# Local attention's projections as three bfloat16 products, with the lookback scores before the phrase keys

## The reference, cut to what matters

```
h = layernorm(x)
q = h @ q_w.T + q_b;  k = h @ k_w.T + k_b;  v = h @ v_w.T + v_b
ph = running mean of h within chunks of 32 tokens      # the phrase state
pk = ph @ pk_w.T + pk_b;  pv = ph @ pv_w.T + pv_b
scores of q against the tokens before it; top 16 of them, with the token just before once more,
    and one phrase score, of q against pk of the token before
w = softmax over these 18;  out = weighted sum of v and pv
x = x + out
```

## Time and profile before

| | |
|---|---|
| median of three runs | 2538.76 us |
| the profiled execution's own time | 2541.76 us |
| its span, first to last instruction | 2539.8 us |
| mean granted TensorE clock over the span | 0.955 of full |
| PE busy | 2312.9 us (91%) |
| DVE, ACT, POOL busy | 1826.2, 1557.3, 1123.5 us |
| first instruction of `local1` | 2375.35 us |
| end of its last instruction (line 2739) | 2474.85 us |

### The profile page before, as it was taken

One profiled execution on the slowest core, in us unless ns is written; L12 is line 12 of the kernel. 1 busy time (PEld: TensorE's weight loads), 2 busy tenths in 40 slices (PEclk: granted clock), 3 DMA queues, 4 the chain that ended last, 5 costly groups with the idle time before them and its releaser, 6 DMA issues. The chain is left out here.

```text
span 2539.8 us, 57508 instructions
## 1 busy us (share of the span) xinstructions
PE 2312.9 (91%) x21955; PEld 1499.9 (59%) x21955; DVE 1826.2 (72%) x3370; ACT 1557.3 (61%) x2912; POOL 1123.5 (44%) x895
## 2 busy tenths in 40 slices
PE   5799999999999999998888699995799899998795
PEld 3346656666566655666445577772567676776442
DVE  7478877888788867776363699995777777766236
ACT  4347666666666666665234499883377676887313
POOL 4437666666666665554100000004367676656100
PEclk8899999999999999998899799997999999999897
DMA  6223233224222321124321699984533434224002
GB/s 212 52 71 93 84 106 83 75 75 125 82 70 79 107 72 42 42 60 152 113 104 39 219 368 364 365 301 165 163 110 118 127 121 127 88 89 161 30 1 85
DMA packets 256273, 313.56 MB, mean 123 GB/s; under 512 B 71792, under 2 KB 183024, under 8 KB 255104
## 3 DMA queue, kind: packets, MB, share of 16 engines
q1 hardware_dynamic: 252048, 301.76, 37.1%
q10 hardware_dynamic: 3312, 6.03, 0.6%
q0 software_dynamic: 640, 2.10, 0.3%
HBM read 226.23 MB, written 47.91 MB: 108 GB/s over the span
## 5 line engine op out<-in xcount | busy, mean ns | idle before, releaser
L816 POOL TENSOR_TENSOR a_plo<-a_p,a_phi 128x512 bf16<-128x512 f32 x272 | 316.0, 1162 | 358.9 <-ACT a_phi L870 358.1
L1074 PE MATMUL ps<-w,a_xhi 128*128 128x512 bf16 x1088 | 413.9, 380 | 6.0 <-PEq L3010 6.0
L1075 PE MATMUL ps<-w,a_xhi 128*128 128x512 bf16 x1088 | 413.8, 380 | 0.0
L1076 PE MATMUL ps<-w,a_xlo 128*128 128x512 bf16 x1088 | 413.8, 380 | 0.0
L2234 POOL TENSOR_TENSOR a_plo<-a_p,a_phi 128x512 bf16<-128x512 f32 x256 | 306.6, 1198 | 178.8 <-ACT a_phi L2271 169.7
L838 ACT ACTIVATE a_kraw<-ps 128x256 f32<-128x256 f32 x272 | 104.2, 383 | 373.5 <-PE ps L1076 371.8
L2366 DVE CUSTOM_DVE_ANT_0 a_junk<-ps,a_biasrow 128x512 bf16<-128x512 f32 x256 | 176.2, 688 | 117.6 <-PE ps L2506 114.6
L893 DVE TENSOR_TENSOR a_v<-ps,a_v 128x256 bf16<-128x256 f32 x272 | 114.3, 420 | 164.3 <-ACT a_v L840 162.8
L2266 ACT ACTIVATE a_p<-ps,a_mcol 128x512 f32<-128x512 f32 x256 | 174.8, 683 | 87.6 <-PE ps L2524 79.9
L907 DVE SCALAR_TENSOR_TENSOR a_kraw<-a_kraw,a_rn 128x1024 f32<-128x1024 f32 (+1 forms) x80 | 154.2, 1928 | 78.3 <-POOL a_rn L781 78.3
L781 POOL TENSOR_TENSOR a_rn<-a_rn,a_power 128x16 f32<-128x16 f32 (+1 forms) x80 | 204.0, 2550 | 6.6
(11 more groups left out here) (461 smaller groups left out, 6890.6 us busy)
## 6 DMA issues: line engine op xcount, KB each, us to landing
e_wst<-in_L_ffn_W SPq DMA_DIRECT2D x46, 2048.0 KB, 10.3
a_ks<-a_khi SPq DMA_DIRECT2D x256, 64.0 KB, 2.0
a_ks<-a_klo SPq DMA_DIRECT2D x256, 64.0 KB, 2.1
a_ct<-in_ctxT SPq DMA_DIRECT2D x16, 1024.0 KB, 6.3
a_ks<-k1h_d SPq DMA_DIRECT2D x128, 128.0 KB, 2.5
xa<-in_ctx SPq DMA_DIRECT2D x8, 1024.0 KB, 5.6
k1h_d<-a_khi SPq DMA_DIRECT2D x64, 128.0 KB, 2.1
k1l_d<-a_klo SPq DMA_DIRECT2D x64, 128.0 KB, 1.7
```

Source lines behind the costliest of these rows:

```text
L816: pool.tensor_tensor(p_lo[:, m % 3, :], p32[:, m % 2, :], p_hi[:, m % 3, :], ALU.subtract)\
L1074: pe.matmul(out, x_hi[:, c, tile], w_hi[:, c, g, :], start=(c == 0), stop=False)
L1075: pe.matmul(out, x_hi[:, c, tile], w_lo[:, c, g, :], start=False, stop=False)
L1076: last = pe.matmul(out, x_lo[:, c, tile], w_hi[:, c, g, :], start=False, stop=(c == C - 1))
```

## The change

Only `local1` changes.

- Every float32 operand of the projections is split into a high and a low bfloat16 tile: all five weights (`w_hi`, `w_lo`), the turned `Hn` (`ht_hi`, `ht_lo`) and the phrase state (`pt_hi`, `pt_lo`). ACT makes the high tiles (five copies of 128x2048, eight of 128x512), DVE the four `ht_lo` straight from PSUM, POOL the five `w_lo` of 128x2048 and the four `pt_lo` of 128x512.
- The 12 feature groups and the 8 value groups are 12 bfloat16 matmuls of 128x512 each. Scores, turns and outputs stay float32.
- PE's order becomes: queries, keys, lookback scores, phrase keys, phrase scores, four values, the turns of the weights, the first phrase value, four outputs' first halves, and then each further phrase value followed by the second half of the output before it.
- Values use banks 2 and 3 alone. DVE's masking and top 16 follow the lookback scores directly; the phrase scores' part stands behind them. DVE's copies of values and additions into `X` are spread along.

```diff
+        @block.gpsimd
+        def _(pool):
+            def weight_low(k):
+                pool.wait_ge(whi_done, k + 1)
+                pool.tensor_tensor(w_lo[:, k], w[k], w_hi[:, k], ALU.subtract).then_inc(wlo_done, 1)
+
+            for k in range(3):
+                weight_low(k)
+            for c in range(C):
+                pool.wait_ge(pthi_done, c + 1)
+                pool.tensor_tensor(pt_lo[:, c, :], PT_[:, c, :], pt_hi[:, c, :], ALU.subtract).then_inc(ptlo_done, 1)
+            for k in range(3, 5):
+                weight_low(k)
...
         @block.scalar
-            norm.scalar(act)
-            turn.scalar(act, ps, HT)
-            act.wait_ge(c_in, 7 * 16)
-            for n in range(3 * C):
+            def weight_high(k):
+                act.wait_ge(w_in[k], 16)
+                act.activation(w_hi[:, k], w[k], ACT.Copy).then_inc(whi_done, 1)
...
+            weight_high(0)
+            norm.scalar(act)
+            weight_high(1)
+            for c in range(C):
+                act.wait_ge(h_tp, c + 1)
+                act.activation(ht_hi[:, c, :], ps[:, c, :], ACT.Copy).then_inc(hthi_done, 1)
+            weight_high(2)
+            act.wait_ge(c_in, 7 * 16)
+            for n in range(C):
+                feature(n)
+                act.wait_ge(pf_cp, n + 1)
+                act.activation(pt_hi[:, n, :], PT_[:, n, :], ACT.Copy).then_inc(pthi_done, 1)
+            for n in range(C, 2 * C):
+                feature(n)
+                if n < C + 2:
+                    weight_high(3 + n - C)
+            for n in range(2 * C, 3 * C):
+                feature(n)
...
         @block.vector
             norm.vector(dve, step, Hn, X)
+            for c in range(C):
+                dve.wait_ge(hthi_done, c + 1)
+                dve.tensor_tensor(ht_lo[:, c, :], ps[:, c, :], ht_hi[:, c, :], ALU.subtract).then_inc(htlo_done, 1)
...
-            dve.wait_ge(s_mm, 2)
+            dve.wait_ge(s_mm, 1)
             (masking, two rounds of max and match_replace, r1)
+            dve.wait_ge(s_mm, 2)
             (phrase scores, m_ready)
+            value(0)
             dve.wait_ge(e_done, 2 * B)
...
         @block.tensor
+            def features(k):
+                pe.wait_ge(wlo_done, k + 1)
+                if k == 2:
+                    pe.wait_ge(ptlo_done, C)
+                hi, lo = (ht_hi, ht_lo) if k < 2 else (pt_hi, pt_lo)
+                for o in range(C):
+                    n = C * k + o
+                    if n >= 2:
+                        pe.wait_ge(f_cp, n - 1)
+                    out, cols = ps[:, 4 + n % 2, :], slice(o * P, (o + 1) * P)
+                    for c in range(C):
+                        pe.matmul(out, w_hi[:, k, c, cols], hi[:, c, :], start=(c == 0), stop=False)
+                        pe.matmul(out, w_hi[:, k, c, cols], lo[:, c, :], start=False, stop=False)
+                        last = pe.matmul(out, w_lo[:, k, c, cols], hi[:, c, :], start=False, stop=(c == C - 1))
+                    last.then_inc(f_mm, 1)
...
+            pe.wait_ge(hthi_done, C)
+            pe.wait_ge(htlo_done, C)
+            features(0)
+            features(1)
+            scores(0)
+            features(2)
+            scores(1)
+            for b in range(B):
+                value(0, b)
             for k in range(2):
                 pe.wait_ge(w_ready, k + 1)
 ...
+            value(1, 0)
             pe.wait_ge(w_cp, 2)
+            pe.wait_ge(pf_cp, C)
+            for b in range(B):
+                output(0, b)
+            for b in range(1, B):
+                value(1, b)
+                output(1, b - 1)
+            output(1, B - 1)
```

More of the change, by code:

```diff
@@ L2616, in local1 @@
     Hn = sb("l_h", [P, B, D], F32)
-    HT = sb("l_ht", [P, C, TOK], F32)
+    ht_hi = sb("l_hthi", [P, C, TOK], BF16)
+    ht_lo = sb("l_htlo", [P, C, TOK], BF16)
     PT_ = sb("l_pht", [P, C, TOK], F32)
+    pt_hi = sb("l_pthi", [P, C, TOK], BF16)
+    pt_lo = sb("l_ptlo", [P, C, TOK], BF16)
     w4 = sb("l_w4", [P, C, D], F32)
-    w = [keep["lw"][:, k] for k in range(4)] + [w4]
+    w = [keep["lw"][:, k] for k in range(4)] + [w4[:]]
+    w_hi = sb("l_whi", [P, 5, C, D], BF16)
+    w_lo = sb("l_wlo", [P, 5, C, D], BF16)
     bc = sb("l_bc", [P, 3, C], F32)
@@ L2656, in _ @@
         def _(sp):
[L2657 to L2658 removed]
+            for dst, src in ((prefix, "prefix"), (inv, "inv_place"), (lower, "lower"), (shift, "shift"), (bc, "l_bc")):
                 sp.dma_start(dst[:], t[src]).then_inc(c_in, 16)
@@ L2720, in _ @@
             step(last)
+            step(dve.tensor_tensor(r1[:], r2[:], sc[:], ALU.not_equal))
+            step(dve.tensor_tensor(r1[:], r1[:], sh4, ALU.add))
+            dve.wait_ge(s_mm, 2)
+            step(dve.scalar_tensor_tensor(ph[:], p4, D ** -0.5, sh4, ALU.mult, ALU.mult))
+            step(dve.tensor_reduce(z[:, :, 0], ph[:], AX.X, ALU.add))
             step(dve.tensor_tensor(z[:, :, 1], m8a[:, :, 0], z[:, :, 0], ALU.max))
             dve.tensor_scalar(z[:, :, 2], z[:, :, 1], -1.0, None, ALU.mult).then_inc(m_ready, 1)
[L2723 to L2726, removed]
+            value(0)
             dve.wait_ge(e_done, 2 * B)
@@ L2731, in _ @@
             step(dve.reciprocal(z[:, :, 5], z[:, :, 3]))
+            value(1)
             step(dve.tensor_tensor(z[:, :, 6], z[:, :, 4], z[:, :, 5], ALU.mult))
@@ new lines, in scores, with value @@
+            def scores(k):
+                pe.wait_ge(f_cp, C * (k + 2))
+                for b in range(B):
+                    tok = slice(b * P, (b + 1) * P)
+                    for c in range(C):
+                        last = pe.matmul(ps[:, k, tok], qkp[:, 0, c, tok], qkp[:, 1 + k, c, tok],
+                                         start=(c == 0), stop=(c == C - 1))
+                last.then_inc(s_mm, 1)
+            def value(k, b):
+                n = B * k + b
+                if b == 0:
+                    pe.wait_ge(wlo_done, 4 + k)
+                if n >= 2:
+                    pe.wait_ge(v_cp, n - 1)
+                hi, lo = ((ht_hi, ht_lo), (pt_hi, pt_lo))[k]
+                tok = slice(b * P, (b + 1) * P)
+                out = ps[:, 2 + n % 2, :]
+                for c in range(C):
+                    pe.matmul(out, hi[:, c, tok], w_hi[:, 3 + k, c, :], start=(c == 0), stop=False)
+                    pe.matmul(out, hi[:, c, tok], w_lo[:, 3 + k, c, :], start=False, stop=False)
+                    last = pe.matmul(out, lo[:, c, tok], w_hi[:, 3 + k, c, :], start=False, stop=(c == C - 1))
+                last.then_inc(v_mm, 1)
@@ L2744, in _, with output @@
+            def output(k, b):
+                pe.wait_ge(v_cp, B * k + b + 1)
+                mm = pe.matmul(ps[:, 4 + b, :], wT[:, k, b * P:(b + 1) * P], vv[:, k, b, :], start=(k == 0), stop=(k == 1))
+                if k:
+                    mm.then_inc(o_mm, 1)
             pe.wait_ge(norm.done, B)
-            turn.tensor(pe, ps, Hn, identf)
+            for c in range(C):
+                for b in range(B):
+                    last = pe.transpose(ps[:, c, b * P:(b + 1) * P], Hn[:, b, c * P:(c + 1) * P], identf[:])
+                last.then_inc(h_tp, 1)
```

28 lines of the change are left out of this document (13 added, 15 removed).

## The result

The changed kernel took 2523.32 us (median of four runs, 2520.63 to 2526.58), the kernel before beside it 2537.74 (four runs, 2532.03 to 2540.55). The ratio is 0.9944, with a 95% interval of [0.993, 0.9958]: 14.2 us less, between 10.7 and 17.8 (the medians themselves are 14.4 apart). The prediction was 2525 us, 13.6 less, in a range of 2517 to 2531. The profiled execution took 2526.58 us, its span 2524.8.

What follows compares the result with a forecast made beforehand. `local1` was taken as bound first by DVE's and ACT's norm chain, then by PE alone. Terms: -16.8 + 2.9 + 0.2 + 0.95 - 0.9 + 0.1 = -13.6 us, from 2538.76 to 2525, range 2517 to 2531.

Steps and rivals of the forecast that it cites:

- The forecast case: Whole kernel: bfloat16 products save PE time in `local1`, line 86 is held by POOL; 13.6 us less, 2525 us, chance 0.53.
- products, 20 groups: PE in `local1`: 12 feature and 8 value groups take 2.59 us each instead of 3.43, 16.8 us less.
- line 86 held: Norm at the start of `local1`: DVE's line 86 stands still until POOL's first subtraction ends, 2.9 us more.
- `ht_lo` ahead of `PT_`: DVE in `local1`: `ht_lo` delays the first `PT_`, for which PE's third prefix group waits, 0.2 us more.
- second wait for a feature copy: PE in `local1`: it waits twice, not once, for the last copy of a feature group, 0.95 us more.
- wait for the turned weights: PE behind the turns: `value(1, 0)` now covers the wait for ACT's copies, 0.9 us less.
- last output behind a value copy: End of `local1`: the output behind the last value group waits for DVE's 0.69 us copy, 0.1 us of it uncovered.
- The term I looked for longest: What POOL's first split does to DVE's norm in `local1`: 2.9 us more at line 86, bounds 0 and 7.0.
- Rival 1: Norm: line 86 passes and line 90 is held twice, or the table load comes first; 2528 to 2529 us, chance 0.25.
- Rival 2: Norm: nothing of it is held by POOL; 16.5 us less, 2522 us, chance 0.1.
- Rival 3: PE in `local1`: preparation or banks stop it, 6 us or more of new waits; 2531 to 2540 us, chance 0.08.
- Rival 4: PE's bfloat16 groups: the granted clock falls to 0.50, kernel slower, 2575 us with all 20 groups; chance 0.04.

Runs made afterwards that it cites:

- experiment 5: Changed kernel with bfloat16 products and early split kept, but all features, then scores, eight values over six banks, turns, outputs: 2526.42 us in one run.
- Experiment 1: Changed kernel with the first weights' split moved behind the norm's square root (the late split): 2522.09 us (five runs), ratio 0.9935 to the kernel before.
- Experiment 2: Changed kernel without line 86, its constant 1e-5 folded into the bias of ACT's root, early split kept: 2527.88 us in one run.
- the second set: The later of two sets in which the eight follow-up kernels were run; the kernel before beside it took 2537.46 us (eleven runs).
- experiment 3: Two kernels, each the kernel before with POOL work added at the stage's start: one subtraction, 2533.34 us; three memsets, 2542.79 us (one run each).

## Why the prediction was right

The forecast case came true. Its terms against the traces:

| term | predicted, us | measured, us |
| --- | --- | --- |
| products, 20 groups | -16.8 | 2.59 apart for 3.43: -16.9 |
| line 86 held | +2.9 | +2.96 (0.171 to 3.130) |
| `ht_lo` ahead of `PT_` | +0.2 | with the next term +0.8; +0.2 by experiment 5 |
| clock rises later | not in the sum | +0.6 by experiment 5 |
| second wait for a feature copy | +0.95 | +1.05 (0.78, the lost overlap of 0.16, and 0.1) |
| wait for the turned weights | -0.9 | -1.0 (0.74, 0.16 and 0.1) |
| last output behind a value copy | +0.1 | +0.2 |
| sum | -13.6 | -12.9; the stage itself: -12.9 |

The predicted 0.95 for the wait is a small slip: its own numbers, 2430.49 - (2388.35 + 12 x 3.43), give 0.98.

**The term I looked for longest was right in its form and size.** The row of four elements beside a POOL subtraction decided it against the element of line 381 that passed. A step of two in the source made no difference, as the rule of the Trainium skill ("VectorE: DVE Perf Modes", "What auto-detection actually checks") had it, which asks for no step there. Experiment 1 takes the hold away and gets 3.0 us back.

**Rival 1**, line 90 held twice, was a real mechanism and not the case here. Experiment 2 shows it once line 86 is gone: the four instructions are held for 4.7 us in all, 1.0 and 3.7, where I had put 5.9 (2.4 and 3.5). The first hold is shorter because the table load, which ran ahead of line 86's result in the changed kernel, here waited until DVE's statistics were done (2375.24, 1.08 us of waiting). It makes the root and the start of `l_h` late: 4.8 us into the stage and not 3.6.

**Rival 2**, nothing held, is what the late split makes of the change: a stage 16.5 us shorter than before (99.45 - 82.97), the -16.5 that the rival had.

**Rival 3** did not occur, at the point I had called tight. DVE's first value copy ran from 2432.68 to 2433.37, at once behind PE's first value group, and PE's third group, which needs its bank, was due at 2435.07. The second copy, behind the exponentials, ended at 2436.99, and the fourth group was due at 2437.66. So the margins were 1.7 and 0.7 us, where I had put 2 and 1.5: the change got through closer than I had reckoned. PE's only idle time in the window of scores and values is the wait of 0.78 in the middle and the end of the first: of the 1.02 (28.80 - 27.78), 0.92, and the rest lies in gaps of under 0.1.

**Rival 4** needed the clock to fall. From 2389.6 to 2459.45 it was 1.00 in every window above, through two stops of 0.78 and 20 groups that change banks. The Trainium skill's rule on cycling through banks ("TensorE: Matmul & The Clock Gate", "A second HAM failure mode: psum-queue depth-cycling"), which the prediction set against this change, is not borne out here.

**What was mis-sized** is small: the clock. I took the path from the first transpose to the first feature from before, with 0.2 for `ht_lo`. The windows of PE, one microsecond each from the first transpose on (PE busy, number of instructions, PEclk, DMA share, GB/s), first of the kernel before, then of the changed one:

```profile
2383.95:2384.95 1.00, 1.00 (x8) 0.64 0.23 88
2384.95:2385.95 1.00, 1.00 (x11) 1.00 0.02 8
```

```profile
2385.40:2386.40 1.00, 1.00 (x7) 0.50 0.00 0
2386.40:2387.40 1.00, 1.00 (x8) 0.73 0.00 0
2387.40:2388.40 1.00, 1.00 (x10) 1.00 0.00 0
```

A window at 0.64 has spent 0.28 of its microsecond at the full clock. So the clock rose 3.7 us behind the first transpose before (at 2384.67) and 5.5 us behind it after (2386.94). The 32 prefix matmuls, which lie there, take 4.10 us before and 4.88 after; with `ht_lo` in place and the clock's rise at 3.7 (experiment 5) they take 4.27. That divides the 0.8 into 0.2 and 0.6. The kernel with memsets has no `ht_lo` and took 4.82 with the rise at 5.2, so behind a late rise the clock alone may account for all of the 0.8. In the other kernels the rise came between 3.4 and 5.2 us behind the first transpose. It is no property of the change: the kernel of experiment 5 has the changed kernel's instructions up to the first features, and the same hold, and its clock rose at 3.7 us where the changed kernel's rose at 5.5. What decides it no run here shows.

What the run times add is consistent: -14.2 with an interval of -17.8 to -10.7 takes in -13.6 as well as -12.9. That the median came within 2 us of 2525 is in part luck, since eleven runs of the kernel before, beside the second set, spread from 2528.3 to 2543.4. The stage is the sharper test, and there the sum was 0.7 us too good, by the clock.

## What to carry to other kernels

Before you put work on POOL, look for the DVE `tensor_scalar` instructions between SBUF tiles that will run beside it, down to four elements a partition (a single one passed, line 381 in the earlier trace rows): one POOL instruction of 4 us on a chain's way costs up to 4 us, whatever the size of the DVE instruction, and POOL's work is better begun when that chain is done. Short pieces alone are no cure: three memsets of 1.8 us held the chain for 1.4 us, one subtraction of 4.5 us for 1.5. Forms with two sources were not tested. In the trace of before a `tensor_tensor` of 128x1 with both sources in SBUF (line 380, at 23.32) took 1.11 us beside a POOL subtraction, where one of that shape in the changed kernel (line 2976, at 2470.06) took 0.15, so it may be held as well. Taking an instruction off such a chain can make it longer, if that lets POOL in at a worse place. Where a change is worth a few microseconds of thousands, compare lengths of the stage between two fixed instructions in traces, and subtract the piece in which the clock is still low, before believing a difference of one or two.

## What the runs showed of the hardware that I had not expected

- A POOL memset, which reads nothing, holds DVE's `tensor_scalar` as a subtraction does (line 86: 0.61 us and not 0.17; line 90's first: 1.53 and not 0.54).
- A reciprocal of 128x4 between SBUF tiles isn't held: 0.18 us beside a subtraction (experiment 2) and beside a memset (experiment 3), where the `tensor_scalar` of the same shape stands until POOL ends. Statistics and their aggregation beside POOL keep their times as well (in the changed kernel, beside POOL from 2374.86 on: 2.47 us for four statistics and 0.38 for four aggregations, as before).
- The moment at which the granted clock rises after PE starts varied from 3.4 to 5.5 us between nearly equal kernels, by 1.8 us between two with the same instructions up to there, worth up to 0.9 us of this stage (the prefix matmuls took from 3.97 to 4.88).
- The start of the stage varied by 11 us between kernels with the same code ahead of it. What sets that was not looked into.
